# Stacked q and k operands of a decoder layer: rows moved by DMA, or by selection matmuls on TensorE

## The reference

```python
# self attention: one k and v for all heads ("A" in the kernel)
q = (x @ Wq.T + bq) * SCALING;  k = x @ Wk.T;  v = x @ Wv.T + bv
x = layernorm(x + softmax(q k^T) v @ Wo.T + bo)
# causal attention ("B") and attention to a context of 512 tokens ("C"), 16 heads each
y = softmax(where(causal, q k^T * scale, -inf)) v
y = y + softmax(qc kc^T * scale) vc
x = layernorm(x + y @ Wp + bp)
# top-2 of 8 experts, each h = x W1[e]^T + b1[e]; a, b = split(h); g = a * sigmoid(b); g Wo^T + bo
x = layernorm(x + mixture)
```

## Time and profile before

| | |
|---|---|
| median of three runs | 249.64 us |
| the profiled execution | 250.64 us |
| its span | 248.8 us |
| PE busy | 187.5 us (75%) |
| DVE busy | 172.9 us (69%) |
| ACT busy | 91.6 us (37%) |
| POOL busy | 57.8 us (23%) |

### The profile page before, as it was taken

The page is one execution under the profiler, slowest core; times in us unless marked ns, Lnnn a source line. Parts: engine busy times, 40 slices in busy tenths (PEclk is TensorE's granted clock), DMA queues, the critical chain, the costliest instruction groups (busy, mean ns, idle before and its releaser), DMA issues.

```text
span 248.8 us, 3659 instructions
## 1 busy us (share of the span) xinstructions
PE 187.5 (75%) x1280; PEld 93.0 (37%) x1280; DVE 172.9 (69%) x423; ACT 91.6 (37%) x138; POOL 57.8 (23%) x86
## 2 busy tenths in 40 slices
PE   3726708988862585299879999999999987989931
PEld 2411102223341353065324344476556543334411
DVE  4729998893383488338888797988452487996762
ACT  4600004477600020054217384674766423332300
POOL 6299997000281119300000000001000010001111
PEclk9955556999996577569979999999999999999985
DMA  6860796000065627950020200000000000000000
GB/s 156 196 74 10 92 103 63 5 2 2 3 69 52 58 34 83 127 107 32 3 86 0 89 0 2 3 2 5 2 4 3 0 0 3 1 0 12 11 0 22
DMA packets 9126, 9.42 MB, mean 38 GB/s; under 512 B 1492, under 2 KB 7052, under 8 KB 9108
## 3 DMA queue, kind: packets, MB, share of 16 engines
q1 hardware_dynamic: 7668, 6.82, 16.3%
q0 software_dynamic: 1440, 2.37, 8.6%
HBM read 4.02 MB, written 0.26 MB: 17 GB/s over the span
## 4 chain that ended last, share of the span: by engine, by line
PE 45%; DVE 28%; DMA 12%; issue 6%; SPq 4%; ACT 3%; POOL 1%; POOLq 0%; DVEq 0%; ACTq 0%
PE y L528 12%; DVE mneg L695 11%; PE w L452 5%; PE t L497 5%; DMA k_stack_b<-part_k 4%; SPq L378 4%; DVE mpart L703 4%; DVE val_qc L820 4%; DMA q_stack_B<-mrow 3%; DMA q_stack_A<-part_q 3%; PE w L442 2%; PE t L486 2%; PE w L601 2%; PE t L479 2%; PE t L601 1%
## 5 line engine op out<-in xcount | busy, mean ns | idle before, releaser
L695 DVE TENSOR_REDUCE mneg<-w 128x1 f32<-128x512 f32 (+2 forms) x128 | 78.5, 652 | 29.8 <-PE w L452 11.0
L887 ACT ACTIVATE probs<-t 128x1024 f32<-128x1024 f32 x48 | 48.3, 1023 | 54.5 <-PE t L479 31.4
L1001 POOL TENSOR_SCALAR rstd<-mv 128x2 f32<-128x2 f32 (+1 forms) x8 | 1.8, 225 | 161.2 <-DVE mv L645 161.2
L452 PE MATMUL w<-k_stack_c,q_stack_A 128*128 128x512 bf16 x64 | 25.3, 411 | 4.1 <-DVE mneg L695 3.5
L442 PE MATMUL w<-k_stack_a,q_stack_A 128*128 128x256 bf16 x64 | 16.0, 354 | 9.1 <-DMA q_stack_A<-part_q 5.8
L884 ACT ACTIVATE probs<-t 128x768 f32<-128x768 f32 x16 | 12.9, 811 | 22.0 <-PE t L491 22.0
L497 PE MATMUL t<-q_stack_A,k_stack_c 128*128 128x256 bf16 x128 | 20.1, 282 | 0.5 <-ACT probs L887 0.4
L528 PE MATMUL y<-probs,v_c 128*32 128x256 f32 x256 | 19.0, 388 | 0.3 <-issue 0.2
L601 PE MATMUL w<-w1T,xT 128*128 128x512 f32 x32 | 16.7, 605 | 0.6 <-DVE val_qc L820 0.6
L601 PE MATMUL t<-w1T,xT 128*128 128x512 f32 x32 | 16.5, 596 | 0.0
L445 PE MATMUL w<-k_stack_b,q_stack_B 128*128 128x128 bf16 x32 | 8.0, 250 | 10.9 <-DMA k_stack_b<-part_k 7.8
(11 more groups left out here) (169 smaller groups left out, 334.9 us busy)
## 6 DMA issues: line engine op xcount, KB each, us to landing
w1T<-in_w1T SPq DMA_DIRECT2D x8, 256.0 KB, 3.1
k_stack_c<-y_sb POOLq DMA_DIRECT2D x6, 256.0 KB, 11.8
...
```

The costliest lines, as they stand in the source:

```text
L452: last = nc.tensor.matmul(o[:], q[:, head, q0 + qt * P:q0 + (qt + 1) * P], k_stack_c[:, head, b * TC:(b + 1) * TC], start=True, stop=True)
L695: emptied(V.tensor_reduce(out=dst, in_=src, axis=AX.X, op=ALU.max, negate=True), s)
L887: ins = A.activation(dst, o[:], ACT.Exp)
```

## The change

All rows that `make_stack` moved by DMA now come from PE. The stacks are laid out anew: two heads share 128 partitions, each with six terms of eight rows on its half of 64, and the three rows of maxima lie on rows 48 to 50 of a half. For B and C the q operand of a head (`q_heads`) has zeros on the other head's half, and the k operand holds both heads; for A it is the k operand that has the zeros. So each score matmul still contracts over 128 rows, with as many columns as before.

A new step `RS` fills one part of a stack: `select` multiplies a 0/1 matrix `sel` by 32 partitions of a part; 12 such matmuls of 256 columns (or 6 of 512 for the context's k, 3 for A's k) make one fill of `t0` or `t1` (`w` for A's k), which ACT (or DVE for B's k) copies to the stack, adding the ones of the maxima's rows to k. There are 4 RS steps for A's q, 2 for its k, 4 each for B's q, B's k and C's q, and 8 for the context's k. `S` waits for the RS steps of its group. Other differences: `sel` is built on DVE at the start; batch 1's first projections are a step of their own (`SELF`), as is the context's k projection (`KC`); ACT makes a part 0 only, and DVE the other two parts, B's k among them, straight from PSUM; POOL clears in pieces of 256 words and splits the context's k in quarters; the experts' bias is split on POOL instead of DVE; SP sends the maxima's rows in two DMAs. The planner has new costs and urgencies.

```diff
-ONES = float(np.uint32(0x3F803F80).view(np.float32))
-KROWS = 128
-MROW = 64
+HALF = 64
+MROW = 48
 VD = D + 1
 VW = 32
 
-TERMS = ((0, 0, 0), (8, 1, 0), (16, 2, 0), (32, 0, 1), (40, 1, 1), (96, 0, 2))
-STACKED = 16 * len(TERMS)
+TERMS = ((0, 0), (0, 1), (1, 0), (1, 1), (2, 0), (0, 2))
+TERM_RUNS = (((0, 0, 2, 1), (0, 5, 1, 1), (1, 2, 2, 1), (2, 4, 1, 1)),
+             ((0, 0, 3, 2), (1, 1, 2, 2), (2, 5, 1, 1)))
+PAIRS = H // 2
+EVICT = {"kA": "act", "qA": "act", "qB": "act", "kB": "dve", "qC": "act", "kC": "act"}
...
+         "OUT": (0.43, 2.2), "RS qA": (0.85, 1.05), "RS kA": (0.4, 0.95), "RS qB": (0.85, 2.05), "RS kB": (0.85, 1.3),
+         "RS qC": (0.85, 2.05), "RS kC": (0.85, 1.12)}
+SHIFT = 3.4
+PARTS = {"qB": 2.0, "kB": 3.0, "qC": 4.4}
...
-URGENCY = {"S": (1.12, 0.8), "U": (1.05, 0.61), "PV self": 0.6, "PV cross": 0.72, "F": 0.09, "VC": -0.21, "GT": -3.34, "OUT": -3.34}
+URGENCY = {"S": (1.12, 0.8), "U": (1.05, 0.61), "PV self": 0.6, "PV cross": 0.72, "RS": 1.5, "RS kC": -0.5, "SELF": 0.5, "KC": 0.9, "F": 0.09, "VC": -0.5, "GT": -3.34, "OUT": -3.34}
...
             + [("F", b, e, 1) for e in range(3, E)] + [("GT", b, 1), ("OUT", b, 1)] for b in range(B)]
-    streams = [posts[0], posts[1], ends[0], ends[1], shifts, probs, values, scores, [("VC", 0), ("VC", 1)]]
+    first = [("RS", "qA", 0, 0), ("RS", "kA", 0), ("RS", "qA", 0, 1)]
+    second = [("SELF", 1), ("RS", "qA", 1, 0), ("RS", "kA", 1), ("RS", "qA", 1, 1)]
+    context = [("KC",), ("VC", 0), ("VC", 1)] + [("RS", "kC", b, g, j) for b in range(B) for g in range(2) for j in range(2)]
+    streams = [first, second, posts[0], posts[1], ends[0], ends[1], shifts, probs, values, scores, context]
...
-        if k == "S" and s[1] != "A":
-            return [(("PROJ", s[2]), STACK)]
+        if k == "S":
+            p, b, g = s[1:4]
+            if p == "A":
+                return [(("RS", "qA", b, g), 0.1), (("RS", "kA", b), 0.1)]
+            if p == "B":
+                return [(("RS", "qB", b, g), 0.1), (("RS", "kB", b, g), 0.1)]
+            return [(("RS", "qC", b, g), 0.1)] + [(("RS", "kC", b, g, j), 0.1) for j in range(2)]
+        if k == "RS" and s[1] in PARTS:
+            return [(("PROJ", s[2]), PARTS[s[1]] - 4.2)]
+        if k == "RS" and s[1] in ("qA", "kA") and s[2] == 1:
+            return [(("SELF", 1), -1.0 if s[1] == "qA" else 0.1)]
+        if k == "RS" and s[1] == "kC":
+            return [(("KC",), 6.0)]
+        if k == "KC":
+            return [(("RS", "qA", 1, 1), 0.1)]
...
-        q_stack = {p: sb(f"q_stack_{p}", [KROWS, H, N], BF16) for p in "AB"}
-        q_stack["C"] = q_stack["A"]
-        k_stack_a = sb("k_stack_a", [KROWS, N], BF16)
-        k_stack_b = sb("k_stack_b", [KROWS, H, N], BF16)
-        k_stack_c = sb("k_stack_c", [KROWS, H, B * TC], BF16)
+        q_pairs_a = sb("q_pairs_a", [P, PAIRS, N], BF16)
+        q_heads = {p: sb(f"q_heads_{p}", [P, B, PAIRS, 2, T], BF16) for p in "BC"}
+        k_stack_a = sb("k_stack_a", [P, B, 2, T], BF16)
+        k_stack_b = sb("k_stack_b", [P, PAIRS, N], BF16)
+        k_stack_c = sb("k_stack_c", [P, PAIRS, B * TC], BF16)
 
...
+        def stacked(s):
+
+            _, name, b = s[:3]
+            if name == "kA":
+                return [(rows_of(i), k_stack_a[rows_of(i), b, i, :]) for i in range(2)]
+            if name == "kC":
+                g, j = s[3:]
+                return [(slice(0, P), k_stack_c[:, 4 * g + j:4 * g + j + 3:2, b * TC:(b + 1) * TC])]
+            pairs = slice(4 * s[3], 4 * s[3] + 4)
+            if name[0] == "q" and name != "qA":
+                return [(rows_of(i), q_heads[name[1]][rows_of(i), b, pairs, i, :]) for i in range(2)]
+            dst = k_stack_b if name == "kB" else q_pairs_a
+            return [(slice(0, P), dst[:, pairs, b * T:(b + 1) * T])]
...
-        def make_stack(eng, dst, parts, side, key, which=range(3), done=None):
-
-            for part in which:
-                eng.wait_ge(s_parts[key], part + 1)
-                for term in TERMS:
-                    if term[1 + side] == part:
-                        eng.dma_start(dst(slice(term[0], term[0] + D)), parts[:, part, :]).then_inc(done or s_stack[key], 16)
...
+            def select(o, cols, side, j, r, group, values):
+
+                rows = slice(32 * group, 32 * group + 32)
+                return nc.tensor.matmul(o[:, cols], sel[rows, side, j, r, :], values[rows, :], start=(r == 0), stop=(r == 2))
...
+                    if h == 0 and not qt:
+
+                        wait_emptied(pe, ("RS", "q" + part, b, g))
+                        if part == "A":
+                            pe.wait_ge(cleared["kA"], 1)
+                            wait_emptied(pe, ("RS", "kA", b))
+                        elif part == "B":
+                            wait_emptied(pe, ("RS", "kB", b, g))
+                            pe.wait_ge(s_mask, 1)
+                            pe.wait_ge(cleared["qB"], 1)
+                        else:
+                            pe.wait_ge(cleared["qC"], 1)
+                            for j in range(2):
+                                wait_emptied(pe, ("RS", "kC", b, g, j))
...
+                elif kind == "RS":
+                    _, name, b = s[:3]
+                    side = 0 if name[0] == "q" else 1
+                    pe.wait_ge(s_parts["kC" if name == "kC" else f"{name}{b}"], 3)
+                    if name == "kA":
+                        o = ring("w", s)
+                        for r in range(3):
+                            last = select(o, slice(0, T), side, 0, r, 0, parts_of["kA"][:, r, b * T:(b + 1) * T])
+                    elif name == "kC":
+                        _, _, _, g, j = s
+                        o = ring("t", s)
+                        for r in range(3):
+                            for i in range(2):
+                                last = select(o, slice(i * TC, (i + 1) * TC), side, j, r, 2 * g + i,
+                                              part_c[:, r, b * TC:(b + 1) * TC])
+                    else:
+                        g = s[3]
+                        o = ring("t", s)
+                        for j in range(2):
+                            for r in range(3):
+                                for i in range(2):
+                                    c0 = i * 512 + j * T
+                                    last = select(o, slice(c0, c0 + T), side, j, r, 2 * g + i,
+                                                  parts_of[name][:, r, b * T:(b + 1) * T])
                     give(last, s)
...
-                V.tensor_copy(part(1), val).then_inc(done, 1)
+            def split(name, b, o, scale):
+
+                cols = slice(b * T, (b + 1) * T)
+                dve.wait_ge(s_parts[f"{name}{b}"], 1)
+                return V.scalar_tensor_tensor(out=left[name[0]][:, cols], in0=o, scalar=scale, in1=parts_of[name][:, 0, cols],
+                                              op0=ALU.mult, op1=ALU.subtract)
+
+            def split_low(name, b, bias):
+
+                cols = slice(b * T, (b + 1) * T)
+                done, rest_of = s_parts[f"{name}{b}"], left[name[0]][:, cols]
+                V.tensor_scalar(parts_of[name][:, 1, cols], rest_of, bias, None, ALU.add).then_inc(done, 1)
                 dve.wait_ge(done, 2)
-                V.tensor_tensor(part(2), val, part(1), ALU.subtract).then_inc(done, 1)
+                V.scalar_tensor_tensor(out=parts_of[name][:, 2, cols], in0=rest_of, scalar=bias, in1=parts_of[name][:, 1, cols],
+                                       op0=ALU.add, op1=ALU.subtract).then_inc(done, 1)
...
+                elif kind == "RS" and EVICT[s[1]] == "act":
+                    o = restacked(s, wait_full(act, s))
+                    if s[1][0] == "k":
+                        act.wait_ge(s_rows, 1)
+                    if s[1] in ("kA", "qB", "qC"):
+                        act.wait_ge(cleared[s[1]], 1)
+                    for rows, dst in stacked(s):
+                        if s[1][0] == "k":
+                            ins = A.activation(dst, o[rows], ACT.Identity, bias=row_ones[rows, 2:3])
+                        else:
+                            ins = A.activation(dst, o[rows], ACT.Copy)
+                    emptied(ins, s)
...
+            pool.wait_ge(s_parts["kA0"], 3)
+            for p in "BC":
+                for b in range(B):
+                    for n in range(PAIRS):
+                        ins = G.memset(words(q_heads[p][:, b, n, :, :].rearrange("p i q -> p (i q)")), 0.0)
+                ins.then_inc(cleared["q" + p], 1)
...
-                    sp.dma_start(q_stack[part][MROW:MROW + 3, 8 * g:8 * g + 8, b * T:(b + 1) * T],
-                                 mrow[:, mb % NROW, :]).then_inc(s_shift[mb], 16)
+                    for i in range(2):
+                        row = HALF * i + MROW
+                        pairs = slice(4 * g, 4 * g + 4)
+                        if part == "A":
```

(4 more changed lines are left out.)

490 lines of the change are left out of this document (244 added, 246 removed), and 6 rows, old and new, of the table COSTS.

## The result

The changed kernel takes 283.89 us (median of 4 runs, 282.66 to 285.03) against 249.81 for the kernel before; the ratio is 1.137, 95% interval 1.128 to 1.145. The forecast was slower by 10, 260 us with a range to 269. The sign was right, the size was not: it is slower by 34, outside the range. Some executions of a kernel are over 1.5% longer than its fastest; ratios and intervals here are of the others, medians of all.

A forecast was written before the change was run, and what follows sets the result against it. It took no engine as full up to 121.5 us, some 35 us being waits for the stacks. Stages along DVE's row maxima reached 187.3 us, plus 19.7 and 52.6: span 259.6, median 260, range 236 to 269.

The forecast's parts named there:

- both stretches: Before batch 0's first C maximum (73.1 to 102.2 us) and between the batches' C scores (127.1 to 148.3 us).
- the gap: From batch 0's last C maximum to batch 1's first: 21.2 us of PE work and waits, DVE nearly idle.
- Self scores: Stage up to the last self maximum: 53.2 - 9.5 - 2.4 + 0.5 + 1.7, done at 43.5 us.
- one piece as the most that a cast can wait: In the self scores: a DVE cast waits for one POOL piece at most, so 9.5 us are gained, 0.5 charged.
- First B maximum: After the self scores: 8.1 us to batch 0's projection, then 9.8 for splits, selections and copies; at 61.4 us.
- B of batch 0: Batch 0's B scores: 16 maxima at 0.545, two splits, one division, 11.7 us, done at 73.1.
- The wait for C: After 73.1 us: output chain's rest 6.1, ACT's copies and exps 15.3, then 7.7; first C maximum at 102.2.
- C of batch 0: Batch 0's C scores: 32 tiles at 0.63, two splits, 2.5 for the maxima's rows; 24.9 us, to 127.1.
- C and B of batch 1: Batch 1's maxima and splits 33.3, layer norm and xT 1.0, gate 4.7: 39.0 us, to 187.3.
- Rival 3: Selection steps don't run side by side: 1.3 us a step, 12 on the path, 266 us; chance 0.12.
- Rival 4: In the self scores, closely following short POOL pieces still hold the casts: 9.5 us lost again, 270 us; chance 0.05.
- Rival 1: From first B score to last value step PE's work alone sets the pace, over 90% busy: 228 us; chance 0.25.

The follow-up runs named there:

- e1: Changed kernel with two urgencies raised (RS kC -0.5 to 0.9, VC -0.5 to 0.3), no instruction added or removed: 250.15 us, ratio 0.988 to the kernel before.
- e2: Changed kernel with only the urgency of RS kC raised, to 1.5: 277.82 us, ratio 1.096 to the kernel before.
- e7: Changed kernel with POOL's pieces joined (each q stack cleared by one instruction, context's k split in passes of 1024): 287.91 us, ratio 1.149.
- e3: Changed kernel with three selection steps of batch 1 issuing their 12 matmuls three times over: 285.38 us, ratio 1.140.
- e9: Changed kernel with only the urgency of VC raised, from -0.5 to 1.0, so the context's value matmuls go into the self scores: 285.29 us, ratio 1.139.
- e12: Changed kernel with each C score matmul of batch 0 issued twice into the same place: 287.68 us, ratio 1.145.
- e8: Changed kernel with a selection step's matmuls issued one strip of 32 partitions after the other, not in turn: 289.19 us, ratio 1.151.
- e5: e1 with batch 1's selection steps of q for C ahead of those of q and k for B: 241.78 us, ratio 0.964 to the kernel before.
- e14: e5 with the context's value matmuls behind batch 0's four selection steps of C's k (VC urgency 0.6): 240.11 us, ratio 0.960 to the kernel before.

## Why the prediction was right and where it was wrong

**Direction and place: right.** The kernel is slower, and for the reason given. The forecast named both stretches, said that the selection steps of low urgency make them, and had the gap at 21.2 (22.4 measured) with DVE under 20% busy (14%). What it said of PE, over 80% busy there, was not right: 73%. e1 shows that the order makes the loss. What failed is the size, +34 for +10, and it failed in several terms of the sum at once: of the 23.6 us that the span is longer than forecast, 7.8 lie on the way to the first C maximum and 6.0 in the self scores.

**Self scores, +6.0.** Two terms were too small. The context's projection and a selection step were put at 1.7; DVE waited 2.29 and 3.38 us for PE around them:

```profile
18.72 0.69 DVE L794 TENSOR_REDUCE mneg<-w 128x2 f32<-128x512 f32 x1 [2.29 <-PE w L471]
...
24.38 2.09 DVE L794 TENSOR_REDUCE mneg<-w 128x2 f32<-128x512 f32 x3 [3.38 <-PE w L471]
```

The projection's four instructions took 3.78 at 20 us, where matmuls came at half pace, and 1.98 in the kernel before, where they ran at 8.75, ahead of all scores:

```profile
8.75 1.98 PE L419 MATMUL t<-ctx_room 64*128 64x512 f32 x4
```

And the casts: 0.5 was charged for POOL in all. The short DVE instructions behind the first two groups still wait for POOL, as the rows of the changed kernel show, where 0.17 is the time undisturbed:

```profile
26.77 0.59 DVE L804 TENSOR_TENSOR mneg<-mneg,mpart 128x16 f32<-128x16 f32 x1
27.40 0.59 DVE L805 CAST mpart<-mneg 128x16 bf16<-128x16 f32 x1
...
35.17 1.01 DVE L806 TENSOR_TENSOR mpart<-mneg,mpart 128x16 bf16<-128x16 f32 x1
```

The eight instructions of two groups lose 2.6 us: 2.1 more than charged, and with the two waits for PE (5.7 for 1.7) that makes the 6.0. Here each waits for the end of the POOL instruction that runs; the 1.01 meets one of 1.17.

The prediction went further, and took one piece as the most that a cast can wait. That step was wrong, and luck kept it from costing more: e1 and e2 show a DVE instruction held for sixteen pieces. The kernel before shows it too. The cast of the earlier trace rows that starts at 30.75 and takes 7.88 is longer than any POOL instruction beside it; it ends at 38.63, when the two long memsets of the earlier trace rows and two more instructions have ended:

```profile
37.49 0.65 POOL L986 MEMSET v_b<- 128x668 f32 x1
38.09 0.52 POOL L988 MEMSET bias_sel<- 128x512 f32 x1
```

The rule of the Trainium skill (SBUF — State Buffer, section Who interferes with whom) is that the pair is held for a whole instruction while the other engine blocks. The traces agree that the DVE instruction gets free at the end of a POOL instruction (2.95 against 0.35 in e7), but not always at the end of the first one. What the prediction said the trace of before could not tell was thus in part to be read there: one blocked cast can outlast several POOL instructions that follow each other closely.

**First B maximum: right.** 18.8 us from the end of the self scores against 17.9. A selection step took 0.83 to 0.86 up to its copy (0.85 forecast), side by side.

**B of batch 0, +3.1.** The output chain of batch 1 and the values stand among these scores and DVE waited for PE 0.3 to 1.9 us at several of them. In e3's execution, with the same code up to there and the clock granted in full, the last split starts 1.7 earlier, so 1.7 of the 3.1 are clock. From the first B maximum to the last split the changed kernel's trace has 14.2 us, and e2, e3, e7, e9 and e12 all have 12.5.

**The wait for C, +7.8, the step that failed most.** In the forecast's sum "value matmuls 0.6" stood for 16 fp32 matmuls, which took 3.71; one selection at 0.85 stood where the score waits for two, 2.69; and the sum used rows of full clock (transposition 1.08, here 1.94) for a stretch at 0.72. The first is a plain error of counting: the earlier trace rows priced the adds of `v_c` at 0.28 each, but no row of the matmuls that feed them was read. They stood in the trace of before, eight of the sixteen in this row:

```profile
71.48 1.16 PE L459 MATMUL t<-ctx_room 64*128 64x128 f32 x8
```

So 0.6 should have been 2.3 even there, and half clock made it 3.7. Four adds and a division that I had put on the path lie beside it and give 1.9 back. From 107.4 us on, the balance of all this is +5.1. The other +3.3 is the stretch before, where "1.6 of waits" stood for what ACT waits for the selections (5.8 idle for 2.3 in all, as above), and the rest of the output chain took 0.6 less.

**The other stages.** C of batch 0 came out +2.4: about 1.4 are the tiles at half clock, and between its two groups no maximum starts for 4.1 us (131.9 to 135.9), with the second group's last selection and its copy in the chain, where 2.5 was put for the maxima's rows. C and B of batch 1 came out +2.5, which no run takes apart.

The rule of the Trainium skill (TensorEngine Tiling (Array Packing), section PSUM Bottleneck) that tiling does not speed up the emptying of PSUM fits these rows: between two q selections of B 3.06 us pass in the chain, of which 2.05 are the copy. The prediction drew from it that a step costs its copy and not its matmuls, and this did not hold here: 0.86 of matmuls stand in the chain beside the copy, as the next selection waits for the emptied bank.

**Rivals.** Rival 3 (selections in a row, 1.3 us each) did not come. e8 comes nearest to it, with 1.09 a step, and costs about 4 and not 6. Rival 4 did not come in the changed kernel's trace, though 2.6 of its 9.5 did; in the traces of e1 and e2 its mechanism is there, for another 3.6. Rival 1 is what e5 and e14 come near: with the C stacks early, PE is busy 96% of the stretch from 82.9 to 112.6. It was put down as a way in which the changed kernel might go. There PE is busy 83% from 61 us to the last value step, not over 90%: the order has no score to give to DVE in the two long stretches.

**The range.** It was cut from named cases, each with one thing off, and none with several terms too small at once. The eleven stages erred by +24.7 and -1.1.
